# C rows by broadcast transfer for five products on GpSimd, and a later place in the queue for a store

## The reference

```
h = relu(adj @ layernorm(x) @ gcn_w + gcn_b);  h = layernorm(h) * ln_g + ln_b
xc, z = split(h @ w_in)                        # 256 channels each
u   = silu(causal depthwise conv of 4 taps over xc, + conv_b)
dt, B, C = split(u @ w_xp)                     # 8, 16, 16 columns
dt  = softplus(dt @ w_dt + b_dt)
S_t[n] = exp(dt_t * A[n]) * S_{t-1}[n] + dt_t * B_t[n] * u_t    # 16 states n
y_t = sum over n of S_t[n] * C_t[n];  y = (y + u * D_skip) * silu(z)
x1  = x + y @ w_out
out = x1 + lstm_block(layernorm(x1))           # LSTM over 8192 steps, argmax gate, prefix and suffix sums
```

## Time and profile before

| | us |
|---|---|
| three runs | 1696.55, 1697.48, 1701.78 |
| median | 1697.48 |
| the profiled execution | 1698.79 |
| its span, first to last instruction | 1696.9 |
| TensorE busy (matmul) | 1556.1 (92%) |
| VectorE busy | 1482.2 (87%) |
| GpSimd busy | 1041.3 (61%) |
| ScalarE busy | 1005.5 (59%) |
| the queue of SyncE, of ScalarE: share of the 16 DMA engines | 48.8%, 0.6% |

### The profile page before, as it was taken

One profiled execution on the slowest core, in us unless ns is written; L12 is line 12 of the kernel. 1 busy time (PEld: TensorE's weight loads), 2 busy tenths in 40 slices (PEclk: granted clock), 3 DMA queues, 4 the chain that ended last, 5 costly groups with the idle time before them and its releaser, 6 DMA issues. The chain is left out here.

```text
span 1696.9 us, 21136 instructions
## 1 busy us (share of the span) xinstructions
PE 1556.1 (92%) x5282; PEld 791.8 (47%) x5282; DVE 1482.2 (87%) x1687; ACT 1005.5 (59%) x2093; POOL 1041.3 (61%) x471
## 2 busy tenths in 40 slices
PE   6999999999999999999999999999977677999994
PEld 2444344444444434343444444444422225999993
DVE  8416999999999999999999999999996995557998
ACT  2244666667575757576666667575757554555552
POOL 4024788887878778878788787878885651001221
PEclk9999999999999999999999999999988899999997
DMA  8976665757566666665665757566610202000002
GB/s 311 343 253 236 229 213 196 255 169 272 197 241 224 215 242 205 235 214 213 224 229 187 257 171 269 203 237 230 209 47 0 94 6 106 0 0 1 0 0 99
DMA packets 52073, 298.31 MB, mean 176 GB/s; under 512 B 5522, under 2 KB 5522, under 8 KB 19092
## 3 DMA queue, kind: packets, MB, share of 16 engines
q1 hardware_dynamic: 49680, 293.30, 48.8%
q10 hardware_dynamic: 2308, 4.20, 0.6%
HBM read 285.68 MB, written 11.80 MB: 175 GB/s over the span
## 5 line engine op out<-in xcount | busy, mean ns | idle before, releaser
L509 PE MATMUL bank<-ring,xh 128*128 128x512 f32 x2048 | 953.1, 593 | 15.5 <-DVE xh L989 15.0
L890 POOL TENSOR_TENSOR work<-work 128x1024 f32<-128x1024 f32 x210 | 516.6, 2460 | 238.3 <-DVE work L1081 232.0
L1123 DVE TENSOR_TENSOR_SCAN work<-bank,hstate,work 128x512 f32<-128x512 f32 x512 | 627.2, 1266 | 2.7 <-ACT bank L760 1.3
L509 PEld LDWEIGHTS bank<-ring,xh 128*128 128x128 f32 x2048 | 388.4, 190 | 458.3 <-issue 422.3
L760 ACT ACTIVATE bank<-work,a_neg 128x512 f32<-128x512 f32 x512 | 345.6, 688 | 306.2 <-DVE work L1123 305.9
L1073 DVE TENSOR_TENSOR work<-work,bank 128x1024 f32<-128x1024 f32 x256 | 309.5, 1214 | 60.0 <-PE bank L446 46.3
L446 PE MATMUL bank<-bc_parts,sel 96*128 96x512 bf16 x512 | 192.9, 385 | 33.3 <-DVE work L1081 25.8
L1081 DVE TENSOR_TENSOR work<-work,bank 128x1024 f32<-128x1024 f32 x182 | 216.2, 1194 | 0.0
L441 PE MATMUL bank<-work,w_sb 128*128 128x512 f32 (+2 forms) x352 | 183.5, 618 | 25.4 <-ACT work L676 11.2
L951 POOL TENSOR_TENSOR work<-work 128x256 f32 x32 | 28.5, 891 | 235.9 <-ACT work L797 235.9
L853 POOL TENSOR_TENSOR work<-work 128x1024 f32<-128x1024 f32 x48 | 113.3, 2361 | 79.9 <-ACT work L658 79.7
(11 more groups left out here) (148 smaller groups left out, 1581.4 us busy)
## 6 DMA issues: line engine op xcount, KB each, us to landing
ring<-adj_t SPq DMA_DIRECT2D x256, 1024.0 KB, 4.8
xh<-x_rows SPq DMA_DIRECT2D x16, 256.0 KB, 6.7
work<-x_t SPq DMA_DIRECT2D x16, 256.0 KB, 4.8
x_scratch<-work ACTq DMA_DIRECT2D x16, 256.0 KB, 5.4
work<-x_scratch SPq DMA_DIRECT2D x1, 4096.0 KB, 13.6
out_t<-work SPq DMA_DIRECT2D x16, 256.0 KB, 2.7
xl_scratch<-work SPq DMA_DIRECT2D x13, 256.0 KB, 2.2
ring<-xl_scratch SPq DMA_DIRECT2D x1, 3328.0 KB, 13.1
```

Of the source, the lines that this page charges most:

```text
L509: last = nc.tensor.matmul(mixed[:, :], xn[:, j, :], a, start=(j == 0), stop=(j == BLK - 1))
L890: nc.gpsimd.tensor_tensor(out=acc, in0=hc[0] if n == 1 else acc, in1=hc[n % 2], op=ALU.add).then_inc(y_added, 1)
L1123: nc.vector.tensor_tensor_scan(hb[s % 2][:, h, :], da[h], dbu[s % 2][:, h, :], hstate[:, HV * s + h:HV * s + h + 1], ALU.mult, ALU.add).th ...
```

## The change

1. `POOL_HC` becomes (1, 3, 8, 10, 14). TensorE spreads no C row for these n outside the drain, and ScalarE copies none. Instead ScalarE stores the 16 C rows of a chunk to DRAM (`c_scratch`) at s = 9 of its `pre` stage, and `load_c` fetches each needed row with a transfer that repeats it over 128 partitions: for n = 1, 3, 8, 10, 14 at s = 0, 2, 6, 8, 12. Two buffers take turns, `c_one` and a new `c_two`.
2. `bias_rows` is now the first two partitions of `c_two`. So their load moves from the start to step 16, behind a wait for GpSimd's last product of the loop, and `fold_bias` moves from the start of step 16 to s = 1.
3. The store of xl is queued before block j = 6, not 2.
4. The waits on `c_ready`, `hc_done` and `c_copied` are counted anew (`c_spreads`).

```diff
-POOL_HC = (3, 8, 10)
+POOL_HC = (1, 3, 8, 10, 14)
+C_LOAD = {0: 1, 2: 3, 6: 8, 8: 10, 12: 14}
...
+def c_spreads(cs, n):
+    if isinstance(cs, int) and cs >= NC - 2:
+        return (DS - len(POOL_HC)) * (NC - 2) + DS * (cs - (NC - 2)) + n + 1
+    return hc_count(cs, n, False)
...
+        c_two = sb("c_two", [P, CH])
+        bias_rows = c_two[0:2, :]
...
-        c_one = carve(CH)
+        c_rows = [carve(CH), c_two[:, :]]
...
-                        if j == 2 and not (isinstance(k, int) and k < 4):
+                        if j == 6 and not (isinstance(k, int) and k < 4):
                             sp.wait_ge(xl_ready, k - 3)
                             sp.dma_start(xl_dram[k - 4], xlc).then_inc(xl_stored, 16)
...
             def step(k, par, adj, pre, scan, post):
-                if isinstance(k, int) and k == NC:
-                    fold_bias()
...
                 def spread_c(n):
-                    if drains(k) and (cs > NC - 2 or n >= 1):
-                        pe.wait_ge(c_copied, hc_count(cs, n - 1, True))
-                    elif n >= 2 and n - 2 in POOL_HC:
-                        pe.wait_ge(c_copied, hc_count(cs, n - 2, True))
-                    else:
-                        wait_hc(pe, cs, n - 2)
+                    if drains(k):
+                        if cs == NC - 2 and n == 0:
+                            pe.wait_ge(hc_done, hc_count(cs - 1, DS - 1, False))
+                        else:
+                            pe.wait_ge(c_copied, DS * (cs - (NC - 2)) + n)
+                    elif n in POOL_HC:
+                        return
+                    elif n >= 2:
+                        wait(pe, hc_done, hc_count(cs, n - 2, False))
+                    elif not (isinstance(cs, int) and cs == 0):
+                        pe.wait_ge(hc_done, hc_count(cs - 1, DS + n - 2, False))
                     spread(c_bank, c_ready, DS + n, 0 if drains(k) else n)
...
                 for s in range(16):
+                    if isinstance(k, int) and k == NC and s == 1:
+                        fold_bias()
...
-            act.dma_start(bias_rows[:, :], lstm_bias).then_inc(bias_loaded, 16)
...
                 cs, q = k - 2, 1 - par
+                if isinstance(k, int) and k == NC:
+                    act.wait_ge(pool_hc_done, len(POOL_HC) * (NC - 2))
+                    act.dma_start(bias_rows, lstm_bias).then_inc(bias_loaded, 16)
...
                     if s == 9:
                         written("dbc")
+                        wait(act, c_stored, 16 * (k - 1))
                         nc.scalar.activation(dbc[0:XPW, :], shared[0:XPW, :], ACT.Copy).then_inc(shared_read, 1)
                         act.wait_ge(shared_read, shared_index("dbc", k, pre, post) + 1)
+                        act.dma_start(c_dram[k - 1], dbc[DS:2 * DS, :]).then_inc(c_stored, 16)
...
+                def load_c(n):
+                    i = POOL_HC.index(n)
+                    b = (par + i) % 2
+                    act.wait_ge(c_stored, 16 * (cs + 1))
+                    wait(act, pool_hc_done, hc_count(cs, n, True) - 2)
+                    act.dma_start(c_rows[b], c_dram[cs, n:n + 1, :].broadcast_to([P, CH])).then_inc(c_row_in[b], 16)
...
-                    if scan and s >= 1 and (drains(k) or s - 1 in POOL_HC):
+                    if scan and drains(k) and s >= 1:
                         copy_c(s - 1)
...
+                    if scan and not drains(k) and s in C_LOAD:
+                        load_c(C_LOAD[s])
                     if pre:
                         pre_part(planned(k, s, "pre"))
...
                 def make_hc(n):
-                    pool.wait_ge(c_copied, hc_count(cs, n, True))
+                    if drains(k):
+                        pool.wait_ge(c_copied, DS * (cs - (NC - 2)) + n + 1)
+                        c = c_sb[n % 2]
+                    else:
+                        i = POOL_HC.index(n)
+                        b = (par + i) % 2
+                        pool.wait_ge(c_row_in[b], 8 * (len(POOL_HC) * cs + (i - b)) + 16)
+                        c = c_rows[b]
```

More of the change, by code:

```diff
@@ L123, in build @@
     x1_dram = nc.dram_tensor("x1_scratch", (NC, P, CH), F32, kind="Internal").ap()
+    c_dram = nc.dram_tensor("c_scratch", (NC, DS, CH), F32, kind="Internal").ap()
     xl_dram = nc.dram_tensor("xl_scratch", (NC, P, CH), F32, kind="Internal").ap()
@@ L150, in build @@
         hstate = sb("hstate", [P, DS * HV])
-        bias_rows = sb("bias_rows", [2, 4 * D])
+        c_two = sb("c_two", [P, CH])
+        bias_rows = c_two[0:2, :]
         first_row = sb("first_row", [2, P])
@@ L265, in build @@
         xt_in = [sem(f"xt_in{i}") for i in range(2)]
+        c_row_in = [sem(f"c_row_in{i}") for i in range(2)]
+        c_stored = sem("c_stored")
         row_sum, row_mean, row_centred, row_sq = sems("row_sum row_mean row_centred row_sq")
@@ L394, in fold_bias @@
                 nc.tensor.matmul(mixed[:, :], less_first[:, :], W("w_ih"), start=True, stop=False)
-                nc.tensor.matmul(mixed[:, :], first_row[:, :], bias_rows[:, :], start=False, stop=True).then_inc(folded, 1)
+                nc.tensor.matmul(mixed[:, :], first_row[:, :], bias_rows, start=False, stop=True).then_inc(folded, 1)
             def step(k, par, adj, pre, scan, post):
-                if isinstance(k, int) and k == NC:
-                    fold_bias()
                 if isinstance(k, int) and k == 1:
@@ L727, in copy_c @@
                 def copy_c(n):
-                    act.wait_ge(c_ready, DS * cs + n + 1)
-                    if drains(k):
-                        act.wait_ge(adj_used, PIECES * NC)
-                        wait_hc(act, cs, n - 2)
-                        dest = c_sb[n % 2]
-                    else:
-                        wait(act, pool_hc_done, hc_count(cs, n, True) - 1)
-                        dest = c_one
-                    nc.scalar.activation(dest, c_bank[0 if drains(k) else n % 2][:, :], ACT.Copy).then_inc(c_copied, 1)
+                    act.wait_ge(c_ready, c_spreads(cs, n))
+                    act.wait_ge(adj_used, PIECES * NC)
+                    wait_hc(act, cs, n - 2)
+                    nc.scalar.activation(c_sb[n % 2], c_bank[0][:, :], ACT.Copy).then_inc(c_copied, 1)
+                def load_c(n):
[4 more added lines that the diff above has]
+                    act.dma_start(c_rows[b], c_dram[cs, n:n + 1, :].broadcast_to([P, CH])).then_inc(c_row_in[b], 16)
                 def save_state(c, n):
@@ L903, in make_hc @@
                         wait(pool, y_added, (DS - 1) * cs + (n - 1))
-                    c = c_sb[n % 2] if drains(k) else c_one
                     nc.gpsimd.tensor_tensor(out=hc[n % 2], in0=hb[n % 2], in1=c.unsqueeze(1).broadcast_to([P, HV, CH]),
@@ L1076, in make_hc @@
                 def make_hc(n):
-                    dve.wait_ge(c_ready, DS * cs + n + 1)
+                    dve.wait_ge(c_ready, c_spreads(cs, n))
                     dve.wait_ge(scan_done, HV * DS * cs + HV * (n + 1))
```

## The result

The kernel with the change takes 1713.76 us (median of 4, 1711.89 to 1715.9), the kernel before on the same chip 1698.28 (1696.55 to 1701.78): a ratio of 1.0094, with a 95% interval of 1.0076 to 1.0111. The forecast was 1690, so both its sign and its range were missed. The profiled span is 1711.5 us against 1696.9, 14.6 more. To follow it, these lines are renumbered: L1073 (the products with B, dbu) is now L1105, L1081 (hc) L1113, L1123 (scan) L1155, L869 (dtu) L895, L905 (hc on GpSimd) L937, L890 (add) L916, L446 (spread) L456, L509 (adjacency) L526, L760 (exps) L784, L750 (copy of the mixed bank) L774, L753 (folded weight) L777, L441 (the other matmuls) L451, L394 and L395 (fold) L406 and L407, L1049 (the y product) L1081, and SyncE's L361 and L363 are L373 and L375. In rows of the experiments a line can lie one or two off, in e4's six.

The account below looks back on a forecast made before the run. VectorE was taken to set the pace, TensorE following closely. Thirteen chunks win 12.3 us, k = 2 wins 1, the drain costs 6: 7.3 us less than the median 1697.48, given as 1690.0, range 1682 to 1702.

Parts of the forecast that it names:

- Border with the jump: VectorE's hc(13) end to the next chunk's first dbu, where the loop jumps back: 5.08 us, a gain of about 0.8.
- part 3: Store of xl queued at j = 6: about 3 us a chunk against part 1 alone, nothing against the kernel before.
- part 1: Two more C products (n = 1 and 14) moved from VectorE to GpSimd: 12.3 us won over thirteen chunks.
- Rival A: It cancels: the jump's cost stays and the drain costs 9, so 1697; chance 0.28, shared with part of another rival.
- Border without the jump: The same stretch where the loop goes on: stays 5.08 us, nothing won, VectorE's gap growing to about 1.5.
- First half: First dbu to the eighth B product: 28.80 us, a gain of 0.63, with VectorE waiting 1.0 before hc(2) for GpSimd.
- Second half: Eighth B product to the next end of hc(13) on VectorE: stays at 44.53 us.
- The chunk of 78.41: One pass of `step`, summed from border, first half and second half: 5.08 + 28.80 + 44.53 us, against 79.04 without a jump.
- k = 2: The chunk with no work of the stage behind it: put at 1 us more won.
- part 2: C rows by broadcast transfers: hidden, cost nothing, landing in 5 to 6 us, with 3.6% more DMA engine load.
- Rival B: Slower: C rows crowd the 16 DMA engines and TensorE waits on the ring, 1718; chance 0.14, shared with another rival.
- part 4: Bias rows sharing a C row's buffer delay the drain's start at k = 16: cost 6 us, ends 4 and 9.

Follow-up runs that it names:

- e4: The changed kernel with SyncE held ahead of block j = 2 until dtu is ready, by a wait and a tiny store, xl's store staying at j = 6: 1698.94 us.
- e2: The kernel before with only the store of xl moved from j = 2 to j = 6: 1710.33 us, ratio 1.0067.
- e9: e3 with the twelve loop steps written out, so no jump back, store at j = 6 and ring not held: 1687.08 us, ratio 0.9936.
- e10: The kernel before with the twelve loop steps written out, nothing else changed: 1690.66 us, ratio 0.9951.
- e1: The changed kernel with the store of xl back ahead of block j = 2, all else as changed: 1752.81 us, ratio 1.0315.
- e3: The changed kernel with the bias rows in a buffer of their own, loaded at the start, and the fold back at the start of step 16: 1707.74 us.
- e5: The changed kernel with both the bias rows apart as in e3 and SyncE's hold as in e4: 1691.70 us, ratio 0.9973.
- e12: e9 run again unchanged in five rounds, side by side with e13: 1686.78 us, ratio 0.9942.
- e6: The changed kernel with only n = 3, 8, 10 on GpSimd, their C rows still by transfer and the store at j = 6: 1715.77 us.
- e11: e3 with the fold matmuls left at s = 1 of step 16, where the change put them: 1706.45 us, ratio 1.0063.
- e13: e10 run again unchanged in five rounds, side by side with e12: 1691.85 us, ratio 0.9965.

## Why the prediction was wrong, step by step

**Border with the jump: the step that failed.** The prediction put it at 5.08, a gain of 0.8 at each of five jumps. It measured 8.60, a loss of 2.73 against 5.87; over the five jumps it was 13.6 us lost, where 4.1 were to be won. That is 17.7 of the 23.8 us by which the time missed. Two sentences carried it. First, in part 3: the move is worth "nothing against the kernel before", for VectorE's gaps "have other causes". SyncE's stall of 14 us was read only as a wait that costs nothing; that the ring stopped behind it, just over the jump, and that something else might need the quiet, was not asked. e2 shows this price alone (+13.3 in the loop), e4 removes it (-12.6). Second, in part 1: the 1.13 of "issue" was timed from VectorE's last row. It goes by the time from scan 15, 3.4 us, so an earlier end of VectorE's work wins nothing there, not even with quiet engines. Rival A had this second half of it and, by the drain, 1697; e4 came out at 1698.94.

**Border without the jump:** 5.08 forecast; 766.97 is VectorE's hc(13), and the border before 694.61 is 5.08 by its window. Right, with a gap of 1.07 ended by dtu where about 1.5 was expected. At the loop's end, behind step 15, it was 4.86 against 5.45.

**First half:** 28.80 forecast. Without a jump before it, it is 29.05 (694.61 to 723.66); after a jump 28.31 (776.76 to 805.07), since a late dbu leaves the others time. Over the thirteen chunks it wins 9.3, 5.6 of it behind jumps, where 8.2 was forecast from 0.63 in each. The sum came out near because the two kinds lie on either side of the forecast, which is luck in part: the 0.75 us more behind a jump goes with the late dbu, and without any jump (e9 against e10) the half wins 0.16. The place was one step off too: GpSimd makes VectorE late at scan 3 (0.67, ended by L937), which overwrites what hc(1) reads, not at hc(2) behind add(1).

**Second half and the whole chunk:** 44.53 forecast, 44.5 measured (723.66 to 768.16). The chunk of 78.41 stands in e9 as 78.42, but by other stretches, as said, and e9's loop is 12.9 us below before's, where 13.3 was forecast, only because the jumps went: e10, without the change, is 9.1 below. k = 2 won 0.4, not 1.

**The transfers (part 2):** hidden, as forecast. The rows of C land in 4.7 us in the one buffer and 4.2 in the other (medians; the last column; before it the KB of each), where 5 to 6 was expected; ScalarE's stores of 16 rows (32 KB) land in 1.6:

```profile
work<-c_scratch ACTq DMA_DIRECT2D x35, 256.0 KB, 4.7
c_two<-c_scratch ACTq DMA_DIRECT2D x35, 256.0 KB, 4.2
```

The queue's share rose from 0.6% to 4.2%, 3.6 points as worked out. Rival B, slower by crowded DMA engines, had the right sign for the wrong transfers: it was not the new rows that did the crowding but the old loads, and it was not TensorE that was late by it but, by the packets of q14, the engines' own instructions.

**The store at j = 6 against part 1 alone:** "about 3 us a chunk". The wait for the ring is 2.87 in e1, but the granted clock of 0.68 behind it raised the price, so that the place at j = 2 costs 39 us net. With the change's two products the old place is worse than the new one, and neither place is a good one; only the hold of e4 has both, a quiet jump and a ring that is filled in time.

**The drain (part 4): right mechanism, size too small.** 6 forecast, 10.6 measured, past the upper end of 9. Mis-sized terms: the fold was put at two matmuls of 2.1 us in all, with up to 1.5 more after a rest. But the bank's copy hung behind the same wait, so it was three pairs, all at half rate: 5.8 us from the first's start to the last's end (1256.72 to 1262.47). The bias rows' own landing has no row in the trace; their pair ran last of the three. Scan 0 began 10.60 behind the dbu; 2.27 is what it needs, so it is 8.3 late, where 1257.7 against 1252.37, 5.3, was worked out. After that the y product took 3.92 us, beside GpSimd's hc(0), against 1.90 without such company. This too was named ("up to 2.4 more") and left out of the value taken. Scan 1 is 9.8 late in all (19.28 behind the dbu, 9.48 before). Removing the wait took 8.1 off the drain (e3). The remaining 2.5 us of e3 against before are no more than drains of the same code differ by, but scan 1 is still 2.5 late in e3 (11.95 behind the dbu), and 2.3 to 2.5 in e5, e9 and e12:

```profile
1261.49 1.23 DVE L1074 TENSOR_TENSOR work<-work 128x1024 f32<-128x1024 f32 x1 [3.12 <-POOL work L917]
```

VectorE waits 3.12 us for GpSimd's add(15), where it was 0.63; hc(14) now stands in GpSimd's queue ahead of it. That this is the moved product's price, which the loop hides and the drain doesn't, is argued: no kernel here moved hc(14) alone.

The Trainium skill (SBUF — State Buffer, on the shared port pair) has a VectorE operation with two SBUF inputs and a GpSimd operation that reads SBUF exclude each other for the whole instruction. The trace agrees: hc(0) ends at 1269.68, 2.18 us after the y product was due to start at 1267.50, and 2.18 + 1.90 is 4.1 against 3.92. In the loop, where the partners of the new products have a PSUM operand, GpSimd's rows stay at 2.34 to 2.39, as by that page they should.

**The sum.** Some steps of the working don't add up, none by much: 1697.48 less 7.3 is 1690.2 and not 1690.0, the drain's chain ends at 1257.5 and not 1257.7, and in rival B five rows of 6.4 us each exceed the free 29 us by 3 and not 2.

## What to carry to other kernels

A stalled queue is also silence on the DMA engines: before moving a wait that "costs nothing", list what runs in its shadow, a loop's jump above all, for the engines' instructions come through the same DMA engines (q14). Look at the jump's gap from the last work that all engines share, not from one engine's last row. And a buffer shared to save space puts a wait into the drain, where what stands behind it isn't hidden and ran at half rate after the rest: count all that is queued behind the waiting instruction, at the slow rate. And when two kernels differ by less than their executions do, compare the stage that was changed, against a partner with the same loop form.

## What the hardware showed that was not expected

- **The jump back.** From scan 15's end to the next chunk's dbu it takes 3.4 to 3.8 us with quiet DMA engines (before, e4) and 5.9 to 6.2 with busy ones (after, e2); ScalarE's two gaps of issue are 3.8 and 3.1 us on average. Written out, the steps show no such gap, at no lower DMA load (0.73 of the engines in e9's chunk). What is shown is that the gap goes with the loads' presence at the jump (e2, e4), and that a q14 packet starts 2.1 us ahead of the dbu each time, late where the loads are there. That it is late because it stood in a queue behind them is argued: no row shows a packet's wait, and once started, those ahead of the dbu take 0.3 to 0.6 us with or without loads.
- **TensorE after a rest.** A pair of matmuls of 1.02 to 1.12 us took 2.04 after a rest of 4.00 (after), 1.91 after 2.29 (e6), and 1.02 after 1.46 (e11), with granted clocks of 0.50, 0.52 and 1.00. In e1 a wait of 2.87 for the ring was followed by a granted clock of 0.68 over 10 us. So the slow pairs ran at the lower of the two clock levels.
- **The LSTM part comes in three lengths**, about 292.3, 293.5 (after and e1) and 296.6 us, for the same instructions. In its first 56 us the granted clock is 0.97 in e9, 0.94 in after and 0.85 in e10 (the last but two column):

```profile
1394.00:1450.00 56.00, 48.78 (x337) 41.57 (x336) 27.29 (x69) 24.37 (x85) 2.77 (x3) 0.85 0.23 80
```

It does not belong to a kernel, though each has one kept trace and e9 and e12, and e10 and e13, happen to agree. The mean granted clock of a whole execution is 0.979 to 0.981 where the kept trace has the short part and 0.973 or 0.974 where it has a longer one (e1 apart, 0.958), and it varies between executions of one kernel: e3's two at 0.979 and 0.98 take 1703.64 and 1704.38 us, its five at 0.972 to 0.976 take 1705.73 to 1708.74; e4's and e5's fall apart in the same way, e11's four don't. That these are the lengths of the LSTM part is inferred, for no trace of them is kept. What decides is open. Until it is known, medians here can differ by about 4 us that no edit made, which is why the stages carry the argument.
